# Fewer columns turned and fewer rows multiplied in a batch's fourth key tile

## What is computed

```python
query, key_, value = proj(q, w_q), proj(k, w_k), proj(v, w_v)      # k = v = ctx_1024
scores = jnp.einsum('bhqd,bhkd->bhqk', query, key_) / jnp.sqrt(D_K)
scores = jnp.where(mask == 0, NEG, scores)
attn = jax.nn.softmax(scores, axis=-1)
out = jnp.einsum('bhqk,bhkd->bhqd', attn, value)
```

## Time and profile before

| | |
|---|---|
| median of 3 runs | 773.29 us (771.12 to 774.63) |
| span of the profiled execution | 772.6 us |
| PE busy | 708.0 us, 92% |
| DVE / ACT / POOL busy | 410.2 / 360.6 / 289.0 us |
| first attention, steady part | about 72 us to 461 us |
| granted TensorE clock there | 1.00 (2.4 GHz) |

### The profile page before, as it was taken

How to read it: one execution, slowest core, us unless ns; L and a number is a source line. 1 busy time by engine, 2 the same in 40 slices (tenths; PEclk the granted TensorE clock), 3 DMA queues, 4 the chain that set the end, 5 groups by cost and what they waited for, 6 DMA issues and landing times.

```text
span 772.6 us, 16928 instructions
## 1 busy us (share of the span) xinstructions
PE 708.0 (92%) x6817; PEld 581.6 (75%) x6817; DVE 410.2 (53%) x938; ACT 360.6 (47%) x665; POOL 289.0 (37%) x259
## 2 busy tenths in 40 slices
PE   1999999999999999999999999999999766999970
PEld 0787788778878887888788977887778554788860
DVE  5834434453344424533543345735368348799965
ACT  2425445453545345535454343533455431599950
POOL 0005135513553255225532453432225132788530
PEclk9999999999999999999999999999999985799995
DMA  8401101220021101110110002021001580999818
GB/s 294 149 1 43 45 2 45 98 91 24 29 98 44 44 2 44 44 39 7 44 44 2 3 3 75 1 79 45 3 29 57 188 303 21 330 394 397 333 52 326
DMA packets 30268, 74.77 MB, mean 97 GB/s; under 512 B 4053, under 2 KB 4437, under 8 KB 29155
## 3 DMA queue, kind: packets, MB, share of 16 engines
q1 hardware_dynamic: 25778, 65.16, 23.6%
q0 software_dynamic: 4400, 8.41, 2.9%
HBM read 66.13 MB, written 13.44 MB: 103 GB/s over the span
## 4 chain that ended last, share of the span: by engine, by line
PE 86%; DVE 6%; DMA 3%; ACT 2%; issue 2%; SPq 0%; POOL 0%; DVEq 0%; POOLq 0%; ACTq 0%
PE bank L188 22%; PE bank L190 21%; PE bank L189 20%; PE bank L194 10%; PE bank L345 4%; PE bank L322 3%; DMA raw<-in_wq 2%; DVE x_sb L1611 1%; PE bank L564 1%; DMA wr<-scratch_ys 1%; PE bank L551 1%; PE bank L665 1%; PE bank L580 1%; DVE wh L1084 1%; DVE stats L1340 0%
## 5 line engine op out<-in xcount | busy, mean ns | idle before, releaser
L1637 POOL TENSOR_SCALAR pp<-pp,rl 128x400 f32<-128x400 f32 x128 | 163.8, 1297 | 234.8 <-DVE rl L1162 234.8
L1217 DVE COPY pt<-bank 128x512 f32<-128x512 f32 x64 | 44.3, 692 | 99.4 <-PE bank L194 99.3
L188 PE MATMUL bank<-chi,wk 128*128 128x400 f32 x256 | 93.5, 365 | 0.0
L844 ACT ACTIVATE pp<-pp,acc 128x400 f32<-128x400 f32 x128 | 79.0, 619 | 28.0 <-DVE acc L1250 27.7
L1250 DVE CUSTOM_DVE_ANT_0 pp<-bank,cap 128x400 f32<-128x400 f32 x128 | 66.8, 569 | 46.5 <-PE bank L322 46.5
L190 PE MATMUL bank<-chi,wk 128*128 128x400 f32 x256 | 88.3, 345 | 0.0
L189 PE MATMUL bank<-clo,wk 128*128 128x400 f32 x256 | 88.3, 345 | 0.0
L188 PE MATMUL bank<-wv,chi 128*128 128x512 f32 x200 | 83.5, 417 | 0.0
L189 PE MATMUL bank<-wv,chi 128*128 128x512 f32 x200 | 78.5, 393 | 0.0
L190 PE MATMUL bank<-wv,clo 128*128 128x512 f32 x200 | 78.5, 392 | 0.0
L761 ACT ACTIVATE pt<-bank 128x512 f32<-128x512 f32 x64 | 38.2, 597 | 76.4 <-PE bank L194 75.3
(11 more groups left out here) (238 smaller groups left out, 1387.4 us busy)
## 6 DMA issues: line engine op xcount, KB each, us to landing
wr<-in_We SPq DMA_DIRECT2D x13, 1024.0 KB, 11.6
craw<-in_ctx SPq DMA_DIRECT2D x16, 800.0 KB, 4.4
raw<-in_We SPq DMA_DIRECT2D x8, 1024.0 KB, 10.5
acc<-in_We SPq DMA_DIRECT2D x6, 1024.0 KB, 11.0
scratch_xn<-acc SPq DMA_DIRECT2D x16, 256.0 KB
wr<-scratch_ys SPq DMA_DIRECT2D x8, 512.0 KB, 7.2
x_sb<-in_x SPq DMA_DIRECT2D x2, 1024.0 KB, 8.5
out_dram<-x_sb SPq DMA_DIRECT2D x8, 256.0 KB, 5.9
```

Of the source, the lines that this page charges most:

```text
L188: pe.matmul(o, lhs[0], rhs[0], start=start, stop=False)
L844: act.activation(frame(p8), frame(p8), ACT.Exp, bias=bias, scale=-1.0, accum_out=total).then_inc(S["a_exp"], 1)
L1217: dve.tensor_copy(pt[:, p8 % 4, :, :].rearrange("p a c -> p (a c)"), at("t", 8 * (n - 1) + p8)[:, :]).then_inc(S["v_pt"], 1)
L1637: pool.tensor_scalar(frame(p8), frame(p8), rl[:, n % 2, p8:p8 + 1], None, ALU.mult).then_inc(S["g_pn"], 1)
```

## The change

The last tile, `i4 = 3`, holds between 16 and 128 of a batch's keys: `400 * (n % 8) % 128 + 16`, which is 16, 32, 48, 64, 80, 96, 112, 128 for n % 8 = 0 to 7. The new helper `keys_in` gives that number, and 128 for the other tiles. `t_part` no longer calls `turn4`: the transpose of a tile loads only its first `keys` columns of `pp` and writes only `keys` partitions of the bank. `pv_part` takes only the first `keys` partitions of `vv` and `pt`. Numbers of instructions, semaphores, banks and copies stay as they are; the copies to `pt` still take all 128 partitions.

```diff
+        def keys_in(n, i4):
+
+            return min(128, CW * (n % 8) % 128 + CW - 128 * i4)
...
-                turn4(pe, at("t", 8 * n + p8), lambda i4: weight_columns(n, p8, i4)).then_inc(S["p_t"], 1)
+                bank = at("t", 8 * n + p8)
+                for i4 in range(4):
+                    keys = keys_in(n, i4)
+                    last = pe.transpose(bank[0:keys, 128 * i4:128 * i4 + 128], weight_columns(n, p8, i4)[:, 0:keys], ident)
+                last.then_inc(S["p_t"], 1)
...
                             g = 2 * half + c
+                            keys = keys_in(n, i4)
                             last = pe.matmul(turned[32 * j:32 * j + 32, g, :],
-                                             vv[:, (25 * (n // 8) + 3 * (n % 8) + i4) % 4, 128 * g + 32 * j:128 * g + 32 * j + 32],
-                                             pt[:, j, i4, 64 * c:64 * c + 64], start=(i4 == 0), stop=(i4 == 3))
+                                             vv[0:keys, (25 * (n // 8) + 3 * (n % 8) + i4) % 4,
+                                                128 * g + 32 * j:128 * g + 32 * j + 32],
+                                             pt[0:keys, j, i4, 64 * c:64 * c + 64], start=(i4 == 0), stop=(i4 == 3))
```

## The result

The changed kernel takes 779.75 us (median of 8 runs, 777.73 to 783.67) against 775.01 us (8 runs, 771.12 to 775.88) for the one before: ratio 1.0074, 95% interval 1.0053 to 1.0094, so 0.7% slower and not 3.2%. The profiled execution has a span of 778.2 us and a time of 779.99 us. In the runs of every kernel the time lies 1.7 to 1.9 us above the span, so the profiled execution of the kernel before (span 772.6 us) was about 1 us slower than its median of 773.29 us and not 0.7 us faster; the forecast was made on the median and isn't moved by it.

A forecast was written before the change was run, and what follows sets the result against it. TensorE's queue was taken to bound the kernel; 19.6 us around narrow transposes plus 5.5 us for fewer rows gave 25.1 us on the 773.3 us median, so 798.4 us, 3.2% slower, range 788 to 808.

The forecast's parts named there:

- Part 2: Transposes of up to 64 columns change the array's shape, with gaps and bare loads around each: 19.6 us slower.
- Part 3: Products with the values on 64 rows or fewer change shape three more times per half: 5.5 us slower.
- What bounds the kernel: First attention: TensorE is busy 388.1 of 389 us, so each nanosecond its queue gains or loses is the kernel's.
- Part 1: Transposes load fewer columns, but the load hides behind the stream: gain 0, at most 6.1 us.
- The rule on modes: Skill's claim, cited for the row cuts: switching tiling mode drains the engine; 32, 64 and 128 rows are different modes.
- F: Only the products with the values change shape, narrow transposes don't: 778.8 us, chance 0.07.
- B: Rows alone in the products with the values are no change of shape: 792.9 us, chance 0.11.
- C: The load sets the transposes' pace and no narrow shape costs anything: 767.2 us, chance 0.06.
- D: Nothing changes, the load being hidden and the shape set by more than operand size: 773.3 us, chance 0.06.
- E: A narrow transpose runs as a plain product with one more stream, 7.0 us on top: 805.4 us, chance 0.10.

The follow-up runs named there:

- e1: Changed kernel with only the transposes narrowed, products with the values taking all 128 rows: 774.39 us, ratio 1.0004 to the kernel before.
- e6: Kernel before, with each fourth transpose of batches 0 to 3 and 8 to 11 a plain product of the narrow piece with the identity: 799.45 us, ratio 1.0338.
- e2: Changed kernel with only the rows of the products with the values cut, transposes full: 778.45 us, ratio 1.0067 to the kernel before.
- e3: Transposes full, fourth tile's products with the values taking at least 96 rows: 774.08 us, ratio 1.0005 to the kernel before.
- e4: Changed kernel with both narrow rounds first in each half of `pv_part`: 776.17 us, ratio 1.0029 to the kernel before.
- e5: Changed kernel with both narrow rounds side by side in the middle of each half of `pv_part`: 777.85 us, ratio 1.0058 to the kernel before.
- e7: As e6, but plain products with all 128 columns: 783.34 us including an extra expert block; first to last product with the values 396.1 us against 388.9 before.
- e8: Each slot turns its fourth, narrow piece first, products with the values taking 128 rows: one run, 774.47 us.

## Why the prediction was wrong, by its steps

The forecast was 25.1 us more, 19.6 from Part 2 and 5.5 from Part 3; the stretch grew by 6.2 us.

- **What bounds the kernel**: right. What TensorE's queue lost in this stage came out in the stretch, but for 0.4 us of a wait.
- **Part 1, nothing gained by shorter loads**: right. Loads down to 90 ns in place of 140, pace unchanged at 0.109 us, e1 at 1.0004. The load rule of the Trainium skill ("TensorE: Matmul & The Clock Gate", "LDWEIGHTS (loading the stationary operand)") does not hold for transposes in this case: from 128 to 16 columns the record loses 50 ns, 0.45 ns a column and not the 0.83 of that rule.
- **Part 2, a change of shape around each narrow transpose, 19.6 us**: this is the step that failed; it measured 0 (no gap in the changed kernel, e1 at 1.0004). The price was sound, as e6 shows with 17.4 us for 60 of the same 64 pieces as plain products, over full plain ones: 0.29 us each, against 19.6 / 64 = 0.31 forecast. The condition was not: I took the width of the stationary operand for the array's shape, from rows that hold only plain products on the narrow side, and let transposes inherit it. In every row that I read the transposes were the full side. The one narrow transpose in the trace, L265, stood alone and could say nothing about its neighbours; I used it for its number of records only.
- **Part 3, rows alone change the shape, 5.5 us**: right in its mechanism (e2, e3) and in its number of changes (e4 and e5 count them), 1 us short in its size: 0.136 us a change measured, 0.114 predicted. The first round of the `pv_part` of the earlier trace rows, cut out of the timeline of PE in the kernel before (a window that ends at 308.7 us):

```profile
308.62 0.26 PE L345 MATMUL bank<-pt,vv 128*32 128x64 f32 x4
```

  Its four records last 0.24 us each (the longest of the earlier trace rows) and 0.26 together, so their starts lie 0.02 us apart in all. I counted the gap from the last of the four as if the next would have followed a whole 0.055 us later, though it would have come 0.035 us later. 48 x 0.022 = 1.1 us.
- **The rule on modes**: what the Trainium skill says ("TensorEngine Tiling (Array Packing)", section "Tiling Modes"), that a switch drains and that 64 and 32 rows are modes of their own, agrees with e2 to e5, at 0.136 us a switch with the bare load.
- **The cases**: F came true, with 0.07 (778.8 forecast on a median of 773.3, 5.5 us over; 4.7 in the medians, 6.2 in the stretch). B, C and D fall with e2, where rows alone change the shape, and C with e1 too, where shorter loads gain nothing. E's plain product does not happen to a narrow transpose; made by hand with full width, 60 of them cost the 7.0 us of e7. The range's ends were rounded outward: by the bounds given, B's lower one is 789 and E's upper one 807, which changes nothing here.

What stays open is which property of transpose mode does this: the runs show that the transposes of 16 to 112 columns, whose streaming side was always 128 columns of the identity, behaved as full ones on both sides. Transposes that stream less, or stand in other strips than the first, were not tried.

## What to carry to other kernels

Before a product's rows or columns are cut to what is needed, look at the shape that its neighbours on TensorE have: 64 rows or fewer between products of 128 cost 0.136 us for each change in and out, and gave nothing back: with the streaming side uncut, fewer rows and fewer stationary columns left the pace as it was. Where the cut is needed, put the cut products side by side, and next to a change of shape that is there anyway (e4 loses 2.3 us of stretch, side by side in the middle e5 loses 4.2, the changed kernel 6.2). A price read from one kind of operation holds for that kind: ask for a row with the same mode on the same side before it is multiplied by 128.

## What the runs showed that I had not expected

- Narrow transposes are free of the change of shape on both sides (e1, e8), though the same pieces as plain products cost 0.29 us more than full ones on average (17.4 us / 60).
- The bare load of a transpose grows with its columns at half the price of a plain one. In e6 the plain pieces' matmul records, one of two with a bare load, are longer by 20 ns for 48 columns more, so 40 ns a bare load, 0.83 ns a column:

```profile
L340 PE MATMUL bank<-cst,pp 128*64 128x128 f32 x32 | 6.9, 298 | 0.0
...
L340 PE MATMUL bank<-cst,pp 128*16 128x128 f32 x32 | 6.3, 278 | 0.0
```

  In e8 a bare transpose load of 16 columns costs 0.01 us where one of 128 costs 0.06, so 0.45 ns a column.
